# A decoder layer with 16 experts: tiles of 128 slots, weights split into memory once, three blocks made one

## What is computed

```
x = layernorm(x + self_attention(x))            # 16 heads of 32, causal, rotary
x = layernorm(x + softmax(x @ ctx.T / sqrt(512), masked) @ ctx)   # 1601 context rows a sequence
s = sigmoid(x @ gate_w.T)                       # 2048 tokens, 16 experts
top = top4(s + expert_bias);  w = s[top] / sum(s[top])
x = layernorm(x + sum_e w_e * swiglu_e(x) + swiglu_shared(x))
swiglu(x) = (silu(x @ wg.T) * (x @ wu.T)) @ wd.T                # 512 -> 256 -> 512
```

## Time and profile before

| | |
|---|---|
| median of three runs | 1545.83 us |
| the profiled execution, its span | 1543.87 us, 1542.1 us |
| PE busy (matmul) | 1364.8 us, 89% |
| VectorE (DVE) busy | 1000.3 us, 65% |
| ScalarE (ACT) busy | 784.7 us, 51% |
| GpSimd (POOL) busy | 476.0 us, 31% |
| mean granted clock of PE | 0.951 of full |
| DMA | 159.81 MB |

### The profile page before, as it was taken

How to read it: one execution, slowest core, us unless ns; L and a number is a source line. 1 busy time by engine, 2 the same in 40 slices (tenths; PEclk the granted TensorE clock), 3 DMA queues, 4 the chain that set the end, 5 groups by cost and what they waited for, 6 DMA issues and landing times. The chain is left out here.

```text
span 1542.1 us, 25698 instructions
## 1 busy us (share of the span) xinstructions
PE 1364.8 (89%) x8773; PEld 1138.9 (74%) x8773; DVE 1000.3 (65%) x1760; ACT 784.7 (51%) x1529; POOL 476.0 (31%) x527
## 2 busy tenths in 40 slices
PE   5899999999998589999999888959999999999950
PEld 5667766766774378888888667758898889898950
DVE  6667676677675564656554377547777777777736
ACT  4777577577577242424233242235565555555623
POOL 0243233234222210100100011126665656566630
PEclk9999999999998789999999989979999999999985
DMA  4200000000000240313220071157988888887658
GB/s 177 110 1 28 1 1 29 1 0 1 1 1 1 86 148 2 128 43 105 67 84 25 1 260 31 43 203 168 250 194 221 231 240 179 205 192 181 114 87 301
DMA packets 59484, 159.81 MB, mean 104 GB/s; under 512 B 8200, under 2 KB 8204, under 8 KB 58640
## 3 DMA queue, kind: packets, MB, share of 16 engines
q1 hardware_dynamic: 38352, 108.73, 20.8%
q0 software_dynamic: 21056, 50.07, 16.6%
HBM read 148.68 MB, written 41.55 MB: 123 GB/s over the span
## 5 line engine op out<-in xcount | busy, mean ns | idle before, releaser
L1691 POOL DMA_INDIRECT acc_rows<-e_y,e_to_row x94 | 174.9, 1861 | 148.7 <-DVE e_to_row L1810 123.9
L436 PE MATMUL proj_ps<-wqkv,x_sp 128*128 128x384 f32 x768 | 173.1, 355 | 10.2 <-DVE wqkv L315 10.2
L1755 DVE TENSOR_TENSOR e_w_sp<-e_w_raw,e_w_sp 128x1024 fp32r<-128x1024 f32 x141 | 168.4, 1221 | 18.3 <-ACT e_w_sp L1711 11.9
L1006 PE MATMUL c_score_ps<-ct,x_t 128*128 128x402 f32 x768 | 160.0, 361 | 0.0
L207 POOL TENSOR_SCALAR_AFFINE_SELECT p_t<-p_t 128x128 f32<-128x128 f32 x256 | 87.8, 355 | 219.8 <-ACT p_t L292 216.1
L1711 ACT ACTIVATE e_w_sp<-e_w_raw 128x1024 fp32r<-128x1024 f32 x141 | 144.2, 1055 | 22.6 <-DMA e_w_raw<-w_experts 22.6
L1025 PE MATMUL c_out_ps<-cr,weigh_t 128*128 128x512 f32 (+1 forms) x624 | 147.3, 394 | 1.4 <-DVE weigh_t L865 1.4
L1832 PE MATMUL e_up_ps<-e_x_t,e_w_sp 128*128 128x256 f32 x1128 | 147.9, 287 | 0.0
L1832 PEld LDWEIGHTS e_gate_ps<-e_x_t,e_w_sp 128*128 128x128 f32 x1128 | 142.6, 190 | 5.9 <-DVE e_x_t L1791 2.0
L1006 PEld LDWEIGHTS c_score_ps<-ct,x_t 128*128 128x128 f32 x768 | 141.3, 194 | 7.2 <-issue 5.3
L1832 PE MATMUL e_gate_ps<-e_x_t,e_w_sp 128*128 128x256 f32 x1128 | 144.0, 283 | 1.6 <-DVE e_x_t L1791 1.6
(11 more groups left out here) (217 smaller groups left out, 2312.7 us busy)
## 6 DMA issues: line engine op xcount, KB each, us to landing
e_w_raw<-w_experts SPq DMA_DIRECT2D x141, 512.0 KB
raw<-ctxT SPq DMA_DIRECT2D x16, 800.5 KB, 4.4
raw<-ctx_rows SPq DMA_DIRECT2D x16, 768.0 KB, 4.7
rows<-x_rows SPq DMA_DIRECT2D x1, 4096.0 KB, 12.2
acc_rows<-r_h_sp SPq DMA_DIRECT2D x1, 4096.0 KB, 17.4
x_rows<-rows SPq DMA_DIRECT2D x4, 1024.0 KB, 13.7
acc_rows<-rows SPq DMA_DIRECT2D x4, 1024.0 KB, 4.2
rows<-acc_rows SPq DMA_DIRECT2D x4, 1024.0 KB, 11.9
```

Of the source, the lines that this page charges most:

```text
L436: mm = nc.tensor.matmul(proj_ps[:, tt, 0:GW], x_sp[:, xs, c, tt * P:(tt + 1) * P], wqkv[:, ws, c, hg * GW:(hg + 1) * GW], start=(c == 0 an ...
L1006: mm = nc.tensor.matmul(score_ps[:, f, 0:MQ], x1_t[:, xs, c, qt * P:(qt + 1) * P], ct[:, cs, c, f * MQ:(f + 1) * MQ], start=False, stop=(c ...
L1691: nc.gpsimd.indirect_dma_start(acc[par], bass.IndirectOffsetOnAxis(ap=to_row[:, par, half:half + 1], axis=0), y[:, par, half, :], None, co ...
L1755: nc.vector.tensor_tensor(w_sp[:, par, part, 1, :], w_raw[:, par, part, :], w_sp[:, par, part, 0, :].bitcast(F32), ALU.subtract).then_inc( ...
```

## The change

- **Tiles.** `SLOTS` goes from 256 to 128 and `TILES` from 47 to 79. All tiles are written out; there is no loop. In a tile the tokens stand in both products: gate and up are one matmul of 512 columns (`packed` lays the weights out so), and h is turned by PE afterwards (`turn_h`).
- **Weights.** The weights of all experts are split once and stored, high and low, in memory (`w_split`, 16 x 3.15 MB). This goes by pieces of 384 columns: load (`fetch`), high, low, store. 104 of the 128 pieces stand in cross attention, the other 24 in routing. The experts then load one expert's split weights at a time into a ring of four slots; PE reads from SBUF which slot a tile uses and how many loads it needs (`place`).
- **Routing.** The plan is made by load and by tile (`line_up`, on DVE). The parts of h are split by ACT and DVE and no longer by GpSimd; marks are made by DVE alone; the shared sums are evicted by ACT; x2 itself is stored as the start of the second sum.
- **Blocks.** `route`, `routed_experts` and `finish_rows` are one block without barriers between them.
- **Cross attention.** The ring of raw context has four slots, the turned x two tiles instead of four, the mask's bias one buffer instead of two; in the first tile of a batch the mask is added behind the scores.

```diff
-SLOTS = 2 * P
+SLOTS = P
+SPLIT_EARLY = 13
+PIECE = 384
+NB = 6
+RING = 4
+XR = 2
...
 # cross_attention
+        def pieces_of(n):
+            if n == NT - 1:
+                return 0, 0
+            if n % TT == TT - 2:
+                return (4, 5) if n + TT > NT else (4, 0)
+            return {0: (0, 4), 1: (4, 6), 3: (4, 5)}[n % TT]
...
+                def pieces(first, last):
+                    for g in range(first, last):
+                        store(g)
+                        if g >= 2 and g - 2 + NB < first_piece[NT]:
+                            fetch(g - 2 + NB)
...
-                    if b >= 2:
-                        pool.wait_ge(scored, (b - 1) * TT)
+                    if b >= 1:
+                        pool.wait_ge(scored, b * TT)
...
+                def hi_piece(g):
+                    act.wait_ge(piece_in[g % NB], 16 * (g // NB + 1))
+                    nc.scalar.activation(piece[:, g % NB, 0, :], piece[:, g % NB, 1, :].bitcast(F32), ACT.Copy
+                                         ).then_inc(piece_hi, 1)
...
+                def lo_piece(g):
+                    dve.wait_ge(piece_hi, g + 1)
+                    nc.vector.tensor_tensor(piece[:, g % NB, 1, :], piece[:, g % NB, 1, :].bitcast(F32),
+                                            piece[:, g % NB, 0, :].bitcast(F32), ALU.subtract).then_inc(piece_lo, 1)
...
 # route, DVE's order behind the marks
+            find_rows()
+            name_experts()
+            line_up()
+            pieces(16, 17)
+            gate_up(3)
+            pieces(17, 18)
+            lo_h(3)
+            pieces(18, 20)
...
 # routed_experts, SP
+            def load(n):
+                expert = sp.value_load(expert_at[0:1, n:n + 1], min_val=0, max_val=E - 1)
+                if n >= RING:
+                    sp.wait_ge(down_done, sp.value_load(free_at[0:1, n - RING:n - RING + 1], min_val=1,
+                                                        max_val=TILES + 1))
+                sp.dma_start(slot_of(n), split_weights(expert)).then_inc(w_in[n % RING], 16)
+                sp.wait_ge(w_in[n % RING], 16 * (n // RING + (n % RING > 0)))
+                sp.sem_inc(loaded, 1)
...
 # GpSimd
+            def scatter(m):
+                if m >= 2:
+                    pool.wait_ge(*added(m - 2))
+                pool.wait_ge(y_done, m + 1)
...
+            gather(0)
+            gather(1)
+            pool.wait_ge(step, ROUTED)
+            expert = pool.value_load(expert_at[0:1, 0:1], min_val=0, max_val=E - 1)
...
+            nc.gpsimd.dma_start(slot_of(0), split_weights(expert)).then_inc(first_in, 16)
...
 # ACT
+            for m in range(TILES):
+                silu(m)
+                if m >= 1:
+                    weigh_y(m - 1)
+                if m + 2 < TILES:
+                    hi_x(m + 2)
+                hi_h(m)
...
 # DVE
+            for m in range(TILES):
+                gate_up(m)
+                if m + 2 < TILES:
+                    lo_x(m + 2)
+                    weigh(m + 2)
+                lo_h(m)
...
 # PE
+            def front(m, needed, slot):
+                pe.wait_ge(x_lo, m + 1)
+                pe.wait_ge(loaded, needed)
+                if m >= 2:
+                    pe.wait_ge(h_done, m - 1)
+                behind = None
+                for c in range(DC):
+                    for n, (xs, ws) in enumerate(PASSES):
+                        mm = nc.tensor.matmul(both_ps[:, m % 2, :], x_t[:, m % 2, xs, c * P:(c + 1) * P],
+                                              weights(slot, ws, c * GU, (c + 1) * GU),
+                                              start=(c == 0 and n == 0), stop=(c == DC - 1 and n == 2))
+                    if c == 1 and m + 1 < TILES:
+                        behind = place(m + 1)
...
+            for m in range(TILES):
+                behind = front(m, *here)
+                if m >= 1:
+                    back(m - 1, before)
+                if m + 2 < TILES:
+                    turn_x(m + 2)
+                turn_h(m)
```

More of the change, by code:

```diff
@@ L753, in _ @@
                 sp.dma_start(mask_u8[:, 0:M], mask[0]).then_inc(mask_in, 16)
[L754 to L764, removed]
+                for n in range(1, RING):
+                    load_next(0, n)
+                for g in range(NB):
+                    fetch(g)
+                for n in range(RING, DC + RING):
+                    load_next(0, n)
+                for n in range(NT):
+                    b, qt = n // TT, n % TT
+                    if qt == 0:
+                        for part in range(DC + RING, LOADS):
+                            load_next(b, part)
+                        if b + 1 < B:
+                            load_mask(b + 1)
+                            for part in range(RING):
+                                load_next(b + 1, part)
+                    pieces(first_piece[n], first_piece[n + 1])
+                    if qt == TT - 2 and b + 1 < B:
+                        for part in range(RING, DC + RING):
+                            load_next(b + 1, part)
+                for slot in range(NB):
+                    sp.wait_ge(piece_out[slot], 16 * len(range(slot, first_piece[NT], NB)))
             @block.gpsimd
@@ L825, in tile @@
                         hi_context(b, DC + 2)
+                    if between:
+                        hi_piece(g)
                     hi_turned(("w", n, 2))
@@ L837, in tile @@
                         exponentials(n + 1)
+                    for k in range(behind):
+                        hi_piece(g + between + k)
                     if qt == TT - 2 and b + 1 < B:
@@ L936, in tile @@
                             lo_context(b + 1, c)
+                    for k in range(behind):
+                        lo_piece(g + between + k)
                     if n in LATE_NORMS:
@@ L1878, in finish_rows @@
-def finish_rows(nc, sem, rows, acc, out):
+        XG = 6
+        YB = 4
+        GU = 2 * I
+        DOWN = DC * GU
+        w = sb("e_w", [P, RING, 2, WE], F32R)
+        x_g = sb("e_x_g", [P, XG, D + E])
+        weight_in = sb("e_weight_in", [P, 2, E])
+        weight = sb("e_weight", [P, TILES])
+        x_t = sb("e_x_t", [P, 2, 2, DC * P], F32R)
+        gated = sb("e_gated", [P, 2, I])
+        h_f = sb("e_h_f", [P, 2, I])
+        h_t = sb("e_h_t", [P, 2, 2, IC * P], F32R)
+        y = sb("e_y", [P, YB, D])
@@ L1881, in finish_rows @@
+def finish_rows(nc, block, sem, rows, acc, out):
     with ExitStack() as ctx:
@@ new lines, in _ @@
+        @block.scalar
+        def _(act):
+            for b in range(B):
+                root(act, b)
+        @block.vector
+        def _(dve):
+            for b in range(B):
+                dve.wait_ge(row_in[b], 32)
+                for t in range(b * TT, (b + 1) * TT):
+                    nc.vector.tensor_tensor(rows[:, t, :], rows[:, t, :], odd_rows[:, t, :], ALU.add
+                                            ).then_inc(summed, 1)
+                for t in range(b * TT, (b + 1) * TT):
+                    dve.wait_ge(summed, t + 1)
+                    gather(t)
+                aggregate(dve, b)
+                normalise(dve, b)
@@ L1939, in decoder_block @@
+        routed_experts(nc, block, sem, w_split, x2_rows, acc, plan, done, ends)
+        finish_rows(nc, block, sem, rows, acc, out)
 def decoder_block(nc, xT, x, ctxT, ctx_rows, mask, wqkvT, woT, rope, w_experts, gate_wT, expert_bias, out):
```

1549 lines of the change are left out of this document (793 added, 756 removed).

## The result

The changed kernel takes 1521.24 us (median of 4 runs, 1514.26 to 1523.63), the kernel before 1544.78 (4 runs, 1541.14 to 1546.02) on the same chip: ratio 0.9844, 95% interval 0.9805 to 0.9883. It is faster, but by 1.6% where 5.7% was forecast, and 1521 lies just above the range of 1432 to 1520. The profiled execution is the fastest of the four: 1514.26 us, span 1512.6.

The account below looks back on a forecast made before the run. PE was taken to bound the experts (97% busy), with DMA close behind. Span 1542.1 + 4 (cross attention) - 18 (routing and start) - 67 (experts) - 6 (end) = 1455, execution 1457 us; range 1432 to 1520.

Parts of the forecast that it names:

- Routing and start: From cross attention's end to the first expert gate matmul: -18 us, bounds -26 and +3.
- Experts: First gate matmul to last down block's end: 79 tiles of 4.95 us plus 1.4 and 5, 397 for 464.2: -67 us.
- the reads: Experts: PE's two register reads per tile, taken as hidden at zero cost; other bound 1.1 us a tile, 87 us.
- the scatter's landing: Experts: 1.6 us issue plus at most 7.5 landing, 9.1, under two tiles (9.9 us), so hidden in the quiet case.
- rival 2: Experts: DMA is the bound, 1480 us; second form, scatters landing in 10 us, 5.8 us a tile, 1524 us; chance 0.16.
- the 5 us for a late weight load: Experts: 5 us added because the twelfth expert's load comes 7 us late if loads take 20 us.
- Cross attention: Stage that takes over 104 of 128 split pieces: +4 us, bounds -3 and +57.
- Rival 3: Cross attention bound by DVE and ACT order, half of DVE's 57 us showing: 1485 us, chance 0.06.
- End: From PE's last expert block to the next block's first load, 12 us becoming 6: -6 us.
- Rivals 1 and 4: Experts, PE: register reads exposed (1500 half, 1531 fully, chance 0.13); reads and register writes exposed, slower than before (1586, chance 0.05).
- rival 1: Experts: PE's register reads exposed, 1500 us if half, 1531 us if fully; chance 0.13.

Follow-up runs that it names:

- e1: Changed kernel with ScalarE's evictions of the shared expert's down blocks put ahead of pieces and the next hidden tile's copy: 1509.13 us, ratio 0.9781.
- e6: e1 with the first increment of the loaded-experts count moved to the start of SyncE's routing program, no longer behind the last pieces: 1501.78 us, ratio 0.9734.
- e4: Changed kernel with eight gather buffers instead of six in the experts: 1504.76 us, ratio 0.9773.
- e5: Changed kernel with weight loads of experts 5 to 16 cut to 32 bytes a partition, output wrong: 1495.55 us, ratio 0.9698.
- e7: Changed kernel with copy and subtraction of cross-attention pieces, from piece 7 on, working on 8 of 384 columns, output wrong: 1508.70 us, ratio 0.9777.
- e8: Changed kernel with fetches of cross-attention pieces, from piece 7 on, cut to 32 bytes a partition, output wrong: 1506.45 us, ratio 0.9769.
- e13: Changed kernel with the edits of e7 and e8 together, output wrong: 1503.00 us, ratio 0.9742.
- e11: Changed kernel with cross attention's four pieces all put behind a tile's own copies (ScalarE) and subtractions (VectorE): 1589.66 us, ratio 1.0313.
- e9: Changed kernel with four times the register reads per tile on TensorE, eight instead of two: 1878.81 us, ratio 1.2116.
- e14: Changed kernel with twice the register reads per tile on TensorE, four instead of two: 1580.51 us, ratio 1.0234.

## Why the prediction was wrong, step by step

- **Routing and start, the step that failed** (-18 forecast, +10.4 measured, 28 of the 58 us missing). The sum listed what comes to VectorE and ScalarE and found idle time enough; it saw a wait of 7 us only at the last shared rows. In a queue the order counts, not the share: three evictions stood behind a copy that waits for VectorE and a fourth behind the last pieces (e1), and the start behind the last pieces in SyncE's queue (e6). With both gone the part takes 126.6 us where 123.8 was forecast. That the first expert's load slows those pieces was not in the sum.
- **Experts** (-67, measured -49.8). TensorE's time per tile was right: 4.78 by the sum, 4.86 measured, under the 4.95 chosen, and the reads are hidden as taken. Mis-sized was the scatter's landing, "at most 7.5" behind its issue, measured up to 13.3 (14.8 from its start) under a weight load; the gather's landing was no term at all. It is rival 2's second form, but in bursts (14 of 79 tiles), not in each as its 1524 us had it, and it reaches TensorE by the gathers, which stand behind the scatters and land late themselves. e4 and e5 give 396.8 and 391.9 us for the forecast 397, and that this fits so well is in part luck: a quiet tile was taken 0.1 us too long, 7 us in all, and the 5 us for a late weight load did not come (among TensorE's waits in this stage there is none for a weight load). Without these two errors the stage would have missed by 29 us, not 17.
- **Cross attention** (+4, measured +15.4, and 19 by the usual 899.6). Within its bounds of -3 to +57, but the value was taken near the low end because the engines had idle time. The real price is engine time and landings together (e7, e8, e13). e11 shows that the pieces' order can cost 65 us there, in part by a chain through SyncE's queue; how much of the 19 us that chain makes was not measured. Rival 3 put half of VectorE's 57 us in the open; a third was.
- **End** (-6, measured -5.5). Right.
- **Rivals 1 and 4.** Refuted for two reads, and the margin is some 0.3 us. The Trainium skill ("TensorE: Matmul & The Clock Gate", section "Architectural detail: the array is 16× 32×32, not 1× 128×128") was cited for a queue of 64 entries. That two reads hide agrees with it. No run tests that depth, and it is not what sets the cover here: four reads do not hide, because the first begins only 1.91 us before the sixth matmul ends, whatever the queue could hold.
- **Chances.** 0.58 for the forecast was too much. Three causes of 28, 17 and 11 us fell to the same side, and each was a wait in an in-order queue that a sum of busy times cannot show. The end of the range, 1520, lay below rival 2's 1524 and rival 1's 1531, and nothing in it held two rivals at once.

## What to carry to other kernels

When work is moved into another stage, write out for each engine what stands behind each new wait, the DMA issuing engine first: an instruction that frees a bank or releases a stage belongs ahead of any that can wait, not behind. Gather ahead by more than the longest landing seen under full load, not by the median. And when one order is mended, look at once for the next wait: e1 removed 32.8 us of waits and made the part 14 us shorter; the other 11 came only with the second edit (e6).

## What the runs showed of the hardware that was not expected

- A scatter with add of 128 rows of 2 KB lands in 5.0 us by median with 3 MB loads beside it and in 4.8 with four of them only (e5), but at longest in 14.8 and 11.6, and over 9.1 us 23 times against 3: such loads stretch the tail, not the median. A gather's median goes from 6.0 to 4.3 us as well.
- A register read from SBUF on TensorE, with the register work behind it, takes 0.63 us in the changed kernel and 0.70 in e9, against 0.55 worked out for SyncE from the earlier trace rows. Two hide behind matmuls that are still running, four do not (e14).
- Identical code ended cross attention anywhere from 896.0 to 906.9 us in eleven executions, with the DMA engines 71% busy there. Whether the kernel before, at 22%, scatters less in this stage was not measured; whole executions of it differ by 4 to 9 us on one chip, those of the changed kernel by 9.
